# Residual add of a Mamba block through TensorE, a later step product, and a normalization behind the side work

## The reference

```python
xr = x @ in_proj_w.T                      # 256 -> 1024
xf, res = jnp.split(xr, [D_INNER], -1)    # D_INNER = 512
xf = silu(causal_conv(xf));  y   = ssm(xf, res, ...)
xb = silu(causal_conv(xf));  y_b = ssm(xb, res, ..., reverse=True)
x  = layernorm(x + (y + y_b) @ out_proj_w.T)
...
# in ssm: delta = softplus(...);  16 states for each of the 512 channels
dA_cum = exp(reverse cumulative sum of delta * A)
xs = cumsum(delta * u * B * dA_cum) / (dA_cum + 1e-12)
y  = einsum('bldn,bln->bld', xs, C) + u * D;   return y * silu(res)
```

## Times and profile before

| | us |
|---|---|
| runs of the kernel before (three) | 5845.51, 5855.48, 5856.24 |
| median | 5855.48 |
| the profiled execution, own time | 5838.37 |
| its span, first to last instruction | 5836.5 |
| TensorE's granted clock, mean of the span | 0.929 |

### The profile page before, as it was taken

How to read it: one execution, slowest core, us unless ns; L and a number is a source line. 1 busy time by engine, 2 the same in 40 slices (tenths; PEclk the granted TensorE clock), 3 DMA queues, 4 the chain that set the end, 5 groups by cost and what they waited for, 6 DMA issues and landing times. The chain is left out here.

```text
span 5836.5 us, 50669 instructions
## 1 busy us (share of the span) xinstructions
PE 5031.1 (86%) x14640; PEld 2563.0 (44%) x14640; DVE 4622.5 (79%) x4109; ACT 4081.5 (70%) x6431; POOL 4362.3 (75%) x2136
## 2 busy tenths in 40 slices
PE   6888888888888888888888878787889787999999
PEld 3444443434343434344444434343434344656578
DVE  6898989898989898989898989898989992222235
ACT  4888888888888888888888888887878883111100
POOL 4898989898989999999999999999998981000000
PEclk8999989898989999999898989898989898999999
DMA  2444434444444444444444444344444442343356
GB/s 88 128 133 127 136 124 134 128 133 128 133 129 129 132 133 131 129 128 133 126 131 128 135 127 134 127 132 131 124 138 124 137 126 78 99 138 122 98 171 216
DMA packets 555604, 755.29 MB, mean 129 GB/s; under 512 B 124091, under 2 KB 272443, under 8 KB 553277
## 3 DMA queue, kind: packets, MB, share of 16 engines
q1 hardware_dynamic: 540765, 737.36, 41.1%
q10 hardware_dynamic: 14560, 14.68, 0.8%
HBM read 662.04 MB, written 89.82 MB: 129 GB/s over the span
## 5 line engine op out<-in xcount | busy, mean ns | idle before, releaser
L643 POOL TENSOR_TENSOR g_ring<-dtu,b_ring 128x1024 f32<-128x1024 f32 x1026 | 2418.9, 2369 | 271.6 <-DVE e_ps L1000 246.1
L1000 DVE TENSOR_TENSOR_SCAN e_ps<-e_ps,g_ring 128x1024 f32<-128x1024 f32 x1024 | 2343.3, 2288 | 11.8 <-POOL g_ring L643 11.8
L1156 PE MATMUL y_ps<-v_ring,ident 128*128 128x512 f32 x3088 | 1626.3, 636 | 235.1 <-DVE res_gate L983 189.9
L652 POOL TENSOR_TENSOR v_ring<-z_ring,c_ring 128x1024 f32<-128x1024 f32 x768 | 1816.7, 2368 | 0.0
L796 ACT ACTIVATE e_ps<-dt,a_neg 128x512 f32<-128x512 f32 x2050 | 1327.9, 680 | 458.1 <-DVE v_own L1022 298.3
L806 ACT ACTIVATE f_ring<-rsum,consts,a_neg_half 128x512 f32<-128x512 f32 x2052 | 1550.9, 805 | 36.7 <-DVE e_ps L1013 33.7
L1156 PEld LDWEIGHTS y_ps<-v_ring,ident 128*128 128x128 f32 x3088 | 589.3, 204 | 889.6 <-issue 807.4
L1013 DVE SCALAR_TENSOR_TENSOR z_ring<-f_ring,e_ps 128x1024 f32<-128x1024 f32 x768 | 935.6, 1218 | 50.8 <-issue 1.7
L1156 PE MATMUL y_ps<-v_own,ident 128*128 128x512 f32 x1028 | 533.8, 614 | 0.0
L1089 PE MATMUL side<-u,conv_diag 128*128 128x512 f32 x1088 | 494.6, 597 | 20.7 <-ACT disp_ring L757 11.3
L1326 ACT ACTIVATE x_act<-x_ps,x_bg 128x512 f32<-128x512 f32 x128 | 87.9, 687 | 570.2 <-PE x_ps L1385 570.2
(11 more groups left out here) (133 smaller groups left out, 5180.1 us busy)
## 6 DMA issues: line engine op xcount, KB each, us to landing
b_ring<-bc_scr SPq DMA_DIRECT2D x1027, 256.0 KB, 3.7
c_ring<-bc_scr SPq DMA_DIRECT2D x1025, 256.0 KB, 3.4
pT_scr<-rowT_ring SPq DMA_DIRECT2D x136, 256.0 KB, 4.1
m_pT<-pT_scr SPq DMA_DIRECT2D x16, 2048.0 KB, 8.5
sT_scr<-sT_ring SPq DMA_DIRECT2D x272, 64.0 KB, 2.8
x_xT<-sT_scr SPq DMA_DIRECT2D x16, 1024.0 KB, 9.3
eo_scr<-x_eo SPq DMA_DIRECT2D x32, 512.0 KB, 5.1
m_eo<-eo_scr ACTq DMA_DIRECT2D x14, 1024.0 KB, 7.1
```

The costliest lines, as they stand in the source:

```text
L643: pool.tensor_tensor(g_ring[:, k], dtu[d][:], both(b_ring[:, k:k + 1]), ALU.mult).then_inc(g_done, 1)
L652: pool.tensor_tensor(v_slot(i), z_ring[:, k], both(c_ring[:, k:k + 1]), ALU.mult).then_inc(v_pool, 1)
L1000: dve.tensor_tensor_scan(e, e, g, 0.0, ALU.mult, ALU.add).then_inc(scan_done, 1)
L1156: pe.matmul(y_ps[:, t % 2], ident[:], v, start=(t % (TILES // PAIRS) < 2), stop=True, skip_group_check=True).then_inc(v_used, 1)
```

## The change

It does three things. TensorE adds x to the output projection: for each of the four row tiles, one more matmul of x1 by the identity starts the accumulation, and the wait for x moves from VectorE to TensorE; ScalarE, in place of VectorE, empties the bank by a Copy into x1. The product dtu comes one tile later (`DTU_LAG` 4) and the set column one tile later (`CUT_LAG` 6), while VectorE's sum stays at lag 3. And ScalarE's `normalize` at tile 29 comes behind the side steps of that tile, no longer ahead of them. The side step of tile 29 is the Tanh of `res3`.

```diff
--- before.py
+++ after.py
@@ -214,7 +214,7 @@
     G_AHEAD, B_AHEAD, C_AHEAD = 2, 3, 1
     SP_LAG, X_STEP = 6, 19
     CUT, A_LEAST = 1e25, 1e-22
-    DTU_LAG, RSUM_LAG, CUT_LAG = 3, 3, 5
+    DTU_LAG, RSUM_LAG, CUT_LAG = 4, 3, 6
 
     EARLY = (21, 53)
     ON_DVE = [i for i in range(STEPS) if i % 4 == 1]
@@ -703,9 +703,11 @@
                 kind, i = TABLE[s]
                 src, free = side[:, at.bank(s)], side_free[at.bank(s)]
                 d = int(kind[-1]) if kind[-1] in "01" else None
-                if lag == (3 if kind in ("conv0", "conv1") else 2) and kind not in ("out", "cols"):
+                if lag == (3 if kind in ("conv0", "conv1") else 2) and kind != "cols":
                     act.wait_ge(side_done, at.done(s))
-                    if kind == "in0":
+                    if kind == "out":
+                        act.activation(x1[:, 2 * i:2 * i + 2], src.rearrange("p (a b) -> p a b", a=2), ACT.Copy).then_inc(free, 1)
+                    elif kind == "in0":
                         if i % 2 == 0 and at.mode == "loop":
                             act.wait_ge(dtu_done, at.now * (NDIR * PAIRS) + (part(1, i) + 1))
                         act.activation(xf_pad[:, i, PAD:], src, ACT.Copy).then_inc(free, 1)
@@ -831,10 +833,10 @@
                             guard(b, t // 2 + F_AHEAD, h)
                     if t == ROUGH_TILE:
                         rough_rstds(b)
+                    for s in range(SLOTS):
+                        side_step(at, s, t - tile_of[s])
                     if t == APPLY_TILE:
                         normalize(b)
-                    for s in range(SLOTS):
-                        side_step(at, s, t - tile_of[s])
             epi = At("epi", None, act)
             for turn in range(len(EPI) + LAGS):
                 if turn == EPI_NORM:
@@ -906,13 +908,6 @@
 
                 kind, i = TABLE[s]
                 src, free = side[:, at.bank(s)], side_free[at.bank(s)]
-                if kind == "out" and lag == 2:
-
-                    if i == 0:
-                        dve.wait_ge(x_loaded, at.seq(s) * 16 + 16)
-                    dve.wait_ge(side_done, at.done(s))
-                    both_t = x1[:, 2 * i:2 * i + 2]
-                    dve.tensor_tensor(both_t, src.rearrange("p (a b) -> p a b", a=2), both_t, ALU.add).then_inc(free, 1)
                 if kind == "res" and lag == 3:
 
                     dve.wait_ge(tanh_done, at.nth(s, ("conv0", "conv1", "res")))
@@ -1102,10 +1097,13 @@
                 elif kind == "out":
                     if i == 0:
                         pe.wait_ge(y_gated, at.seq(s) * 2 + 1)
+                        pe.wait_ge(x_loaded, at.seq(s) * 16 + 16)
                     for t in (2 * i, 2 * i + 1):
+                        rows = bank[:, t % 2 * DM:(t % 2 + 1) * DM]
+                        pe.matmul(rows, ident[:], x1[:, t], start=True, stop=False)
                         for c in range(KI):
-                            mm = pe.matmul(bank[:, t % 2 * DM:(t % 2 + 1) * DM], yg[:, c, t * P:(t + 1) * P], w_out[:, c],
-                                           start=(c == 0), stop=(c == KI - 1))
+                            mm = pe.matmul(rows, yg[:, c, t * P:(t + 1) * P], w_out[:, c],
+                                           start=False, stop=(c == KI - 1))
                 elif kind == "xnT":
                     if i == 0:
                         pe.wait_ge(xn_normed, at.seq(s) + (1 + CR))
```

## The result

| | before | after |
|---|---|---|
| runs (four each), us | 5845.51 to 5856.24 | 5793.84 to 5799.28 |
| median, us | 5852.56 | 5798.16 |
| profiled execution, own time, us | 5838.37 | 5799.28 |
| span, us | 5836.5 | 5797.5 |
| granted clock, mean | 0.929 | 0.932 |

The ratio is 0.9907 (0.989 to 0.9924), a gain of 54.4 us. Forecast were 29.2 us, with a range that ended at 5800: the sign was right, the size and the range were not.

A forecast was written before the change was run, and what follows sets the result against it. Three roads per sequence, of VectorE, GpSimd, and ScalarE with TensorE, bound the kernel. 15 sequences x 2.0 us, 0.8 in the first and a serial end of +1.7 and -0.1 gave -29.2 us: 5826.3 us, range 5800 to 5849.

The forecast's parts named there:

- What bounds the kernel: Three roads per sequence: step-18 maximum to step 50 mostly VectorE's, to L117 GpSimd's, then to the maximum ScalarE's and TensorE's.
- The residual add: Steps 7 and 8 shorten by 0.8 us, off the road: 0 in 15 sequences, -0.8 us once in the first.
- The later product: GpSimd's road, step 50 to L117: dtu no longer waits for dt, gaining 1.5 us per sequence.
- The later normalization: ScalarE at tile 29: the Tanh leaves the road behind L117, so step 16's decay comes 0.48 us sooner.
- What would show it: Signs expected in the new trace: changed waits at L919, scan 16, GpSimd and L117, and sequences of about 294 us.
- the sum: Whole kernel: 15 sequences x 2.0, first sequence 0.8, serial end +1.7 and -0.1; together -29.2 us.
- an offset: The profiled execution of before, 5838.4 us, lies 17.1 us under the median; the forecast added this to 5809.2.
- (C): Rival: TensorE's clock changes fall a little better, some 0.8 us a sequence, 5815 us; chance 0.18.
- (B): Rival: TensorE's clock stays high behind L117, the maximum comes 2.7 us sooner still, 5785 us; chance 0.09.
- (D): Rival: GpSimd doesn't keep the 1.5 us and L117 stays; only 0.5 a sequence left, 5849 us; chance 0.14.
- (E): Rival: ScalarE's wait for `out1` delays the decay of step 10 and scan 10; slower, 5888 us; chance 0.06.
- Theory K: Experiments' theory: TensorE's clock drops, at steps 18 and 36 above all, fix sequence lengths; small changes switch length or do nothing.

The follow-up runs named there:

- GpSimd's pauses: Seven or fourteen one-column GpSimd products in step 12: changed kernel 1 and 54 us slower; seven in the kernel before, ratio 0.9985.
- the split: Changed kernel with the x1 half of `normalize` moved from tile 29 to tile 35; 5758.37 us, ratio 0.9857.
- w18b: Changed kernel with zero-column matmuls in TensorE's idle time, four in tile 31 and five in tile 33; 5795.53 us, ratio 0.9906.
- the filled kernels: Zero-column matmuls in tiles 31, 33 and 68: changed kernel (4, 5, 3) 5743.6 us, kernel before (8, 5, 3) 5745.61 us.
- before + 1.0: Kernel before with seven one-column GpSimd products (1.0 us) in step 12 of each sequence; ratio 0.9985.

## Why the prediction was wrong

- **What bounds the kernel: right but for one stretch.** L117 to xn to e to scan 16, and L117 to the transposes to the logits to the maximum, are where the product, the normalization, GpSimd's pauses and the split acted first. But the stretch from the maximum to step 50 isn't "mostly VectorE's": in step 36 VectorE waits 5.57 us for TensorE, and there the time moved too.
- **The residual add: right.** 0 in 15 sequences and 5852.84 measured. Scan 10 didn't wait: the only waits for e from the second sequence on are the one per sequence at step 16. The Copy took 597 ns in the median of 34 (573 to 599), where the row of L711 gave 584. The estimate from the Trainium skill (ScalarE: Activation LUTs, What ACT_TABLE_LOAD costs) was 612. The Trainium skill (ScalarE: Activation LUTs, Rules for kernel authors) also sends add and mul to VectorE; in this kernel moving the work to ScalarE neither cost nor brought anything (0.9998).
- **The later product: right in its mechanism.** GpSimd's 4.86 us for dt are gone, and it stands 3.34 for scan 50 (forecast: some 3). g, times C and dtu are done 10.76 us behind the start of scan 50 before and 9.24 after, the 1.5 of the forecast. At steps 15 and 18 this part alone gave 2.0 us, not 1.5.
- **The later normalization: right.** Scan 16 waits 1.88 us for e (forecast 2.3), xn 0.65 for L117 (forecast 1), the transposes stand behind 3.56 us of idling (forecast 4 to 5). Nearly all that "What would show it" asks for is there, and sequences are 293.55 against "about 294".
- **The step that failed is the sum**, the term "15 sequences x 2.0 = 30.0". It took the size of the gain at the maximum for the size of the gain of a sequence, and so put a change of TensorE's clock behind the maximum at nothing. The maximum's 2.2 us are there; behind it step 36 gave 1.4 more, as TensorE's clock was 0.95 in it and not 0.80. The term measured 15 x 3.41 = 51.2 of the 55.1 us between the spans 5852.6 and 5797.5; the first sequence gave 1.8 (forecast 0.8), and the stretch behind the last scan is 2.3 shorter where I had added 1.6, whose reason I didn't look for.
- **What I took for an offset was in good part the same thing.** Of the 16.1 us between the two spans of before, 9.5 are shorter sequences 1 to 14, and 4.0 the first one. The sequence that I read, 295.68 long, is one of the three whose step 36 took 8.66 us at a clock of 0.96. Sequence 6 after is 293.61 long: 2.07 less, just the 2.0 of the working, since in this pair step 36 hardly differs. Multiplied by 15 it fails, as most sequences of before are 1.3 us longer than the one shown: from 296.96 to "about 294" it is 3, which is 44 us. That the sequences differ stood in the trace, and in the list of runs the slower two are 10 and 11 us from the fastest.
- **The rivals.** (C), the clock's changes falling better, was the right one, at 0.8 us a sequence where it was 1.4, and looked for behind L117, where the clock even fell (step 18: 0.76 to 0.72). Its place is step 36, for which the forecast has no row. (B) didn't come: the clock was 0.62 from 1921.5 to 1936.0, where the earlier trace rows gave 0.61, and TensorE had 4.58 us of idling before the logits. (D) didn't either, GpSimd kept its gain; nor (E).

Theory K stands in what it says of single steps, which the windows show, and in that equal costs are worth 0 or 50 us. It didn't foretell sizes: w18b gained 3 us where it gave at least 40. The lengths at which sequence after sequence stays lie evenly: 296.96 and 293.55 are 3.41 apart, the mean of the pairs of 295.15 and 295.35 is midway, and the means of the filled kernels, 290.1, are 3.4 further down. Why the loop settles there, and why one program changes between two levels from run to run, no run here settles. That step 36 takes less time at a higher clock, its windows and instructions show, and that the clock at such places is worth up to 100 us, the fillings. That the clock is higher in it because the idle in front falls elsewhere is argued from the traces, not tested by itself.

## What to carry to other kernels

A saving on the critical path of a loop is worth its own size only where TensorE's clock does the same afterwards: before summing, list every place at which another engine waits for TensorE and read its granted clock, not only in the stretch of the change. If such places sit at a mixture of two levels, give the forecast steps of the size of a place (here 1.4 to 3 us a turn) as its range, and compare with several turns and runs of before, not one. Filling the idle in front of them with as much harmless work as fits is worth trying first: here it brought the kernel before 100 us, more than the change, and step 36 took the same 7.33 us in every sequence. Filling only one of the places brought nothing.

## What the runs showed of the hardware

- The same 2.74 us of TensorE idling was followed by a clock of 0.80 over step 36 in one kernel and of 0.95 in the other; with the idle filled down to 0.16 us it was 1.00 in every sequence. The step took 10.31, 8.73 and 7.33 us. The Trainium skill (TensorE: Matmul & The Clock Gate, Why this matters for your kernels) asks for no long idle between bursts of matmuls; the trace agrees, and filling such idles took the kernel before from 5845.83 to 5745.61 us on one chip.
- The Trainium skill (TensorE: Matmul & The Clock Gate, Part 1: The HAM clock gate) puts the penalty of the ramp, told there of the start of a kernel, under 1% of a typical span and advises not to fit a count of slow matmuls. Here the drops come back in every turn of a loop, and filling the idles in front of three of them was worth 0.9% of the changed kernel and 1.7% of the kernel before.
- Two microseconds more per sequence on GpSimd cost 54 us, one cost 1 us; and one and the same program (before + 1.0) ran at 5799.4 to 5805.7 us three times and at 5854.6 to 5856.9 us seven times.
